# Attention over heads on one Trainium2 core: shift rows sent ahead of the load of a later group, and value matmuls of 512 columns in place of two of 256

## The reference

```
# wide (16 heads); nested: 8 heads, and weights cut to a few columns by token block
q, k, v = x @ Wq.T, x @ Wk.T, x @ Wv.T            # each split into heads
scores  = einsum('bqhd,bkhd->bhqk', q, k)         # 1024 x 1024 for each head and sequence
attn    = softmax(scores, axis=-1)
out     = einsum('bhqk,bkhd->bqhd', attn, v) @ Wff.T + bff
```

## Time and profile before

| | |
|---|---|
| three timed runs | 3966.51 us median (3959.99 to 3967.83) |
| profiled execution | 3942.5 us, span 3940.8 us |
| PE busy | 3134.1 us (80%) |
| DVE busy | 2798.9 us (71%) |
| ACT busy | 1870.5 us (47%) |
| mean granted TensorE clock | 0.836 |
| L855, nested, idle before it on a DMA of shift rows | 134.8 us |
| L855, wide, idle before it on a DMA of shift rows | 129.5 us |

### The profile page before, as it was taken

How to read it: one execution, slowest core, us unless ns; L and a number is a source line. 1 busy time by engine, 2 the same in 40 slices (tenths; PEclk the granted TensorE clock), 3 DMA queues, 4 the chain that set the end, 5 groups by cost and what they waited for, 6 DMA issues and landing times. The chain is left out here.

```text
span 3940.8 us, 56234 instructions
## 1 busy us (share of the span) xinstructions
PE 3134.1 (80%) x19914; PEld 1771.7 (45%) x19914; DVE 2798.9 (71%) x4370; ACT 1870.5 (47%) x3233; POOL 443.1 (11%) x495
## 2 busy tenths in 40 slices
PE   6658788848777778865878888986999788849998
PEld 4433233412222222233323346665777555537776
DVE  5657677488777777835767733437999777769998
ACT  2215567517666667831656651212444444414443
POOL 0230000040000000023000000112222100031222
PEclk9857889868888889975888976876999888859999
DMA  0051211030000000005121100011111000011111
GB/s 24 15 123 18 33 18 18 5 88 10 17 17 17 17 17 13 6 15 123 18 33 17 18 10 14 1 37 27 46 43 44 22 1 0 0 45 49 45 45 53
DMA packets 70168, 114.65 MB, mean 29 GB/s; under 512 B 13360, under 2 KB 29776, under 8 KB 69968
## 3 DMA queue, kind: packets, MB, share of 16 engines
q1 hardware_dynamic: 69968, 111.97, 12.0%
HBM read 85.72 MB, written 25.43 MB: 28 GB/s over the span
## 5 line engine op out<-in xcount | busy, mean ns | idle before, releaser
L729 DVE TENSOR_REDUCE nested_a_halves<-banks 128x2 f32<-128x1024 f32 x512 | 617.7, 1222 | 237.2 <-PE banks L825 234.0
L729 DVE TENSOR_REDUCE wide_a_halves<-banks 128x2 f32<-128x1024 f32 x512 | 594.7, 1217 | 191.0 <-PE banks L825 190.8
L779 ACT ACTIVATE nested_a_p<-banks 128x512 f32<-128x512 f32 x1024 | 555.0, 597 | 285.2 <-PE banks L855 269.6
L779 ACT ACTIVATE wide_a_p<-banks 128x512 f32<-128x512 f32 x1024 | 555.4, 598 | 198.6 <-PE banks L855 187.5
L1652 ACT ACTIVATE mix_e_h<-banks,mix_b_folded 128x512 f32<-128x512 f32 x512 | 353.5, 690 | 391.9 <-PE banks L1665 385.4
L1616 DVE TENSOR_TENSOR mix_e_h_low<-mix_e_h,mix_e_h_high 128x512 fp32r<-128x512 f32 x512 | 463.9, 906 | 17.5
L855 PE MATMUL banks<-nested_q_stack,nested_k_stack 50*128 50x512 f32 x1024 | 265.2, 445 | 144.2 <-DMA nested_q_stack<-nested_a_shift_rows 134.8
L855 PE MATMUL banks<-wide_q_stack,wide_k_stack 50*128 50x512 bf16 x1024 | 233.9, 399 | 149.2 <-DMA wide_q_stack<-wide_a_shift_rows 129.5
L868 PE MATMUL banks<-nested_a_p,nested_values 128*32 128x256 f32 x4096 | 350.9, 424 | 0.0
L868 PE MATMUL banks<-wide_a_p,wide_values 128*32 128x256 f32 x4096 | 341.4, 413 | 0.0
L825 PE MATMUL banks<-nested_k_stack,nested_q_stack 48*128 48x512 f32 x1024 | 282.4, 546 | 38.2 <-DVE nested_a_halves L729 19.8
(11 more groups left out here) (367 smaller groups left out, 4473.8 us busy)
## 6 DMA issues: line engine op xcount, KB each, us to landing
mix_e_gate<-mix_gates_t SPq DMA_DIRECT2D x128, 256.0 KB, 3.1
nested_q_stack<-nested_q_parts SPq DMA_DIRECT2D x96, 128.0 KB
nested_q_parts<-nested_p_q_cut SPq DMA_DIRECT2D x16, 512.0 KB
nested_k_parts<-nested_p_k_cut SPq DMA_DIRECT2D x16, 512.0 KB
nested_k_stack<-nested_k_parts SPq DMA_DIRECT2D x32, 256.0 KB
wide_q_stack<-wide_q_parts SPq DMA_DIRECT2D x192, 32.0 KB
nested_k_stack<-nested_k_parts SPq DMA_DIRECT2D x32, 128.0 KB
mix_w_w<-L_ffn_w_t SPq DMA_DIRECT2D x2, 2048.0 KB, 9.7
```

The lines of the kernel that those rows point to most:

```text
L729: dve.tensor_reduce(halves[:, half, i, 2 * a:2 * a + 2], bank[:, at:at + 2, :], AX, ALU.max).then_inc(maxed, 1)
L779: act.activation(p[:, kt % 4, j, :], bank[:, ST + n % RING, :], ACT.Exp, scale=scale).then_inc(probs, 1)
```

## The change

Two edits in `attend_stage`. In SP's program `shift_load(u)` stands ahead of the wait and the load of group u/2 + 2, where it stood behind them. In TensorE's program `mix_values` returns at once for c = 0 and does all 512 columns for c = 1: half as many matmuls, each twice as wide. The wait on `probs` moves with them to the second half-step.

```diff
                 for u in range(UNITS):
+                    shift_load(u)
                     if u >= 2 and u % 2 == 0 and u // 2 + 2 < hd.total:
                         sp.wait_ge(shifted, u * ITEMS)
                         hd.load(sp, u // 2 + 2)
-                    shift_load(u)
...
                 def mix_values(u, kt, c):
                     if c == 0:
-                        pe.wait_ge(probs, u * ITEMS + kt * G + G)
-                    if kt == 0 and c == 0:
+                        return
+                    pe.wait_ge(probs, u * ITEMS + kt * G + G)
+                    if kt == 0:
                         wait_past(pe, mix_copied, u)
-                    cols = slice(c * P * 2, (c + 1) * P * 2)
                     for j in range(G):
-                        last = pe.matmul(bank[32 * j:32 * j + 32, MIX, cols],
-                                         hd.values[:, u // 2, kt, 32 * j:32 * j + 32], p[:, kt % 4, j, cols],
-                                         start=(kt == 0 and c == 0), stop=(kt == TILES - 1 and c == 1))
-                    if c == 1:
-                        last.then_inc(mixed, 1)
+                        last = pe.matmul(bank[32 * j:32 * j + 32, MIX, :], hd.values[:, u // 2, kt, 32 * j:32 * j + 32],
+                                         p[:, kt % 4, j, :], start=(kt == 0), stop=(kt == TILES - 1))
+                    last.then_inc(mixed, 1)
```

## The result

| | before | after |
|---|---|---|
| timed runs, median | 3963.25 us (3937.68 to 3967.83, 4 runs) | 3734.0 us (3731.48 to 3740.81, 4 runs) |
| profiled execution | 3942.5 us, span 3940.8 | 3735.9 us, span 3734.2 |
| mean granted TensorE clock | 0.836 | 0.868 |

The ratio is 0.9437 (95% interval 0.9394 to 0.948): 229 us less by the medians, 207 us less by the two profiled executions. Against the two other sets of runs of before, with medians of 3951.21 and 3945.87 us, it would be 217 and 212 us. Both edits did what was forecast, with opposite signs.

A forecast was written before the change was run, and what follows sets the result against it. TensorE was taken to bound nested by a tenth of a microsecond a half-step, with VectorE level in wide. -331 + 101 = -230 us gave a median of 3736 us (3966.5 - 230), range for 8 in 10: 3650 to 3815.

The forecast's parts named there:

- Edit 1, -331 us: Shift rows ahead of the load in SP's queue end 23 TensorE stalls: 264 us of waits plus 67 us of clock.
- the load's queue would be empty in time: SP's load, issued beside TensorE's work, clears before the odd unit's shift rows with 2 to 4 us in hand, costing nothing.
- Edit 2, +101 us: Whole value matmuls expose TensorE's wait for ScalarE's ring: units 1.9 us longer in wide, 1.4 in nested, 101 us lost.
- Wide's chain: A wide key tile on TensorE: 1.07 (ring) + 0.31 (to value block) + 1.01 (block) + 0.22 (scores) = 2.61 us, against 2.22.
- the sum: Both edits over the whole kernel: -331 + 101 = -230 us, 3712.5 us for an execution like the profiled one.
- irregular rest of a unit: Turns and irregular time of a unit beside its eight key tiles, taken as 1.5 us in wide and 1.3 in nested.
- The offset to the median: The profiled run was 24 us under the timed median, so the whole kernel's median was put at 3966.5 - 230 = 3736.
- the merge gains: Rival: the value blocks' ring wait is hidden, a unit up to 1.0 us shorter, 3573 to 3605 us; chance 0.12.
- the collision: Rival: the load's transfers, beside working engines, make odd units' shift rows land late, 3866 us; chance 0.05.
- the stall that stays: Rival: SP reaches shift_load no earlier, so only the wider value matmuls act, 4068 us; chance 0.02.
- The clock's case: Rival: TensorE's short halts in each key tile and at unit starts make the clock fall, up to 4041 us; chance 0.04.
- 1.00 throughout both stages: The profile after would show TensorE's granted clock at 1.00, or 2.4 GHz, throughout nested and wide.

The follow-up runs named there:

- edit 1 alone: Against the kernel before, only shift_load moved ahead of the load in SP's program, value matmuls still in two halves of 256 columns: 3612.26 us, ratio 0.915.
- edit 2 alone: Against the kernel before, only the value matmuls made 512 columns wide, the load still ahead of the shift rows: 4061.49 us, ratio 1.0292.
- the two runs built on it: On edit 1 alone, the ring of 3 banks runs on from unit to unit: 3590.27 us; with ScalarE's mix copy also one exponential later: 3555.61 us.

## Why the prediction was right

**Edit 1, -331 us: measured -339.** The step was to price a stall by the excess of its stretch over clean units, clock and all, and not by the 264 us of the waits alone. The run of edit 1 alone has the clean units of before behind the first two of each stage and no wait on shift rows, which shows it. That the load's queue would be empty in time for the odd unit's rows held as well.

**Edit 2, +101 us: measured +110 alone** (4061.49 against 3951.21), and 122 as the difference of after and edit 1 alone. The rule of the Trainium skill (TensorEngine Tiling (Array Packing), Key Properties: a change of the tiling mode drains TensorE) was right in its sign as far as it goes. The block is 0.13 us a key tile cheaper (2 x 0.57 against 1.00 to 1.01); that this is the drain, no run here separates. The result went the other way because the block was also ScalarE's time. Wide's chain was right to the hundredth: 2.61 us forecast, 2.61 measured. Three runs show that it is the ring: with one item moved at the same width the chain from item to item is still 1.07 us, and the key tile is shorter by just the scores that left the chain; the old halves at the new place bring the loss in full; and a ring of two banks brings the same kind of wait to the old order, in wide in the size that the chain gives.

**What the sum left out.** The four profiled executions, cut at the turns (us; one execution each):

| | before | edit 1 | edit 2 | both |
|---|---|---|---|---|
| first to last turn, three stages | 1637 | 1312 | 1730 | 1406 |
| last turn to last value block, three stages | 90 | 79 | 107 | 106 |
| all else | 2214 | 2219 | 2216 | 2223 |

Between the turns edit 1 gives -325 and edit 2 +93 or +94, near the forecast's -331 and +101. But edit 2 costs another 18 to 26 us in the last units of the stages, behind the last turn, which the sum put at nothing. The forecast for an execution like the profiled one, 3712.5 us, was 23 us too low against the 3735.9 measured, 16 of them in these last units.

**Terms that were off, and made up for each other.** In nested I forecast 2.76 us for a key tile, it is 2.84: the third item doesn't go at 0.57 us but leaves together with the fourth, 1.08 us behind the first pair, and from this pair to the block are 0.43 us and not 0.34. The irregular rest of a unit was 22.05 - 8 x 2.61 = 1.2 us in wide and 23.70 - 8 x 2.84 = 1.0 us in nested, where I took 1.5 and 1.3. So nested lost 1.7 us a unit (1.4 forecast) and wide 1.55 (1.9): 30 x 1.7 + 31 x 1.55 = 99 us, as far as clean units go. Why the third item of a nested key tile waits for the fourth is open: it needs a bank that has long been free. Its weight load takes 186 ns against 95 ns in wide, and in some wide key tiles the two leave together too.

**The offset to the median.** I put the difference of the profiled execution on the median of the timed runs, 3736 against 3734.0. So near a hit is luck: before's own median was 3963, 3951 and 3946 us in three sets of runs, and the forecast was held against the highest of them; by the other two the gain is 217 and 212 us and not 230.

**The rivals.** That the merge gains is refuted by edit 2 alone, the collision by edit 1 alone, the stall that stays by the waits. The clock's case is there in a small form, below; "1.00 throughout both stages" did not hold.

## What to carry to other kernels

Ask of each instruction what runs beside it before it is made larger or moved: with a ring of 3 banks between two engines, the distance of item n and item n+3 on the first engine has to cover the second engine's whole turn of an item, and a long instruction between them was that cover. Merging two blocks of matmuls gains only the fixed part of a block, 0.13 us here, and bunches what stands between them. Look at the last round of a loop by itself: with nothing of a next unit to fill it, the same waits weigh more there. On a DMA queue that is worked off in order put the small transfer that the next step needs ahead of the large one that it doesn't; price the stall by whole units with and without it, since the clock that falls in it is part of its price.

## What the runs showed of the hardware

With the merged value blocks the granted clock fell now and then without a long wait. Windows of the changed kernel, a wide unit without and one with such a place, and the place itself:

```profile
996.40:1018.50 22.10, 19.75 (x141) 4.92 (x137) 19.78 (x22) 17.68 (x34) 0.00 (x0) 1.00 0.00 1
1018.50:1041.80 23.30, 21.20 (x141) 5.09 (x137) 19.77 (x22) 17.69 (x34) 0.00 (x0) 0.93 0.14 35
...
1032.10:1035.40 3.30, 3.30 (x16) 0.54 (x8) 1.80 (x3) 1.62 (x4) 0.00 (x0) 0.50 0.09 17
```

The mean clock of the second is 0.93, and the unit is 1.2 us longer. Of the changed kernel's 61 units from turn to turn four at the stages' starts are slow anyway (0.50 to 0.95); of the other 57 five have such a fall, 6.5 us in all. The clean units of before stand at 1.00, but for one right behind its longest stall (0.95). In edit 1 alone it was 1.00 over 13 nested and 28 wide units:

```profile
351.20:637.00 285.80, 279.46 (x2603) 119.07 (x2599) 263.96 (x272) 238.40 (x443) 0.00 (x0) 1.00 0.19 30
852.40:1426.50 574.10, 545.12 (x5600) 176.99 (x5600) 544.45 (x589) 514.31 (x952) 0.00 (x0) 1.00 0.08 20
```

All five falls lie in units with a load, but the load isn't the cause: the run with both halves together has four such falls, all in units without one. What the nine have in common is the place. Each begins 1.8 to 2.0 us behind the wait for ScalarE at a unit's start (0.3 to 0.5 us of standing still). The other units have the same wait at the same place, and what sets off the one fall and not the others no run here shows.

The larger part lies at the end of each stage, where the last unit runs without score pairs of a later one. From the last turn to the end of the last value block, first nested run, the changed kernel and edit 1 alone:

```profile
656.10:694.80 38.70, 35.27 (x153) 10.43 (x148) 1.36 (x4) 22.92 (x44) 0.00 (x0) 0.69 0.00 1
636.90:663.90 27.00, 26.12 (x249) 10.90 (x244) 1.36 (x4) 23.32 (x45) 0.00 (x0) 1.00 0.01 2
```

In the changed kernel the clock fell 7 us behind the last turn, after waits of 0.45 and 0.59 us for ScalarE, and stayed at 1.2 GHz for 24 us. It fell there in 10 of 12 such ends in the four runs with the value matmuls in one place per key tile, and in 3 of 12 in before, edit 1 alone and the two runs built on it with a ring of three banks (in 2 of 3 with the ring of two). That the waits for the ring set it off fits this; it was not tested by itself. It also resembles what the Trainium skill describes (TensorE: Matmul & The Clock Gate, "A second HAM failure mode: psum-queue depth-cycling"): short idle times between groups of matmuls, from cycling through PSUM banks, that make the clock swing. Here the falls cost some 6 us within the stages. At their ends the changed kernel takes 26 us more than edit 1 alone; the end of wide kept its clock in both and differs by 3.2 us, so by my estimate (26 - 3 x 3.2) some 17 of the 26 are the clock. The forecast's rival had hundreds.
